# Softplus straight from PSUM and a stacked x projection, in the selective scan of a vision kernel

## The reference, cut to what matters

```
# xs: [B, 4, 256, L]; for each direction k
x_dbl  = x_proj_w[k] @ xs                    # 40 rows: 8 for the step, 16 B, 16 C
dt     = softplus(dt_proj_w[k] @ x_dbl[0:8] + dt_bias)      # the steps, 256 x L
B, C   = x_dbl[8:24], x_dbl[24:40]
h[t]   = exp(dt[t] * A) * h[t-1] + dt[t] * u[t] * B[t]      # 256 x 16 states
y[t]   = sum_n h[t, n] * C[t, n]  + D * u[t]
```

## Time and profile before

| | |
|---|---|
| time, median of 3 runs | 17439.1 us (17406.28 to 17441.4) |
| the profiled execution's own span | 17434.3 us |
| the scan's first and last Softplus table load | 5723.8 and 16927.9 us |
| ACT: Exp into a decay slot, mean of one | 772 ns |
| DVE: scan, mean of one | 1203 ns |

### The profile page before, as it was taken

The page is one execution under the profiler, slowest core; times in us unless marked ns, Lnnn a source line. Parts: engine busy times, 40 slices in busy tenths (PEclk is TensorE's granted clock), DMA queues, the critical chain, the costliest instruction groups (busy, mean ns, idle before and its releaser), DMA issues. The chain is left out here.

```text
span 17434.3 us, 303249 instructions
## 1 busy us (share of the span) xinstructions
PE 14999.7 (86%) x109786; PEld 10888.3 (62%) x109786; DVE 15172.8 (87%) x19332; ACT 14292.4 (82%) x28231; POOL 11441.1 (66%) x7881
## 2 busy tenths in 40 slices
PE   8999999997349788888888888888888888888888
PEld 5666666673113566666676676666666666666664
DVE  6777777347989899999999999999999999999995
ACT  5666666334545899999999999999999999999998
POOL 1111111000110799999999999999999999999998
PEclk9999999888679999999999999999999999999999
DMA  1000000112224333333333433333333333334336
GB/s 64 12 16 16 12 16 12 62 38 64 68 59 160 138 122 122 116 120 120 124 133 134 134 131 127 133 125 122 122 118 120 120 126 131 134 134 133 128 125 243
DMA packets 810527, 1801.57 MB, mean 103 GB/s; under 512 B 201328, under 2 KB 432208, under 8 KB 803280
## 3 DMA queue, kind: packets, MB, share of 16 engines
q1 hardware_dynamic: 809040, 1782.17, 30.4%
HBM read 1505.11 MB, written 276.82 MB: 102 GB/s over the span
## 5 line engine op out<-in xcount | busy, mean ns | idle before, releaser
L1832 DVE TENSOR_TENSOR_SCAN sc_h<-ps,sc_dBu 128x512 f32<-128x512 f32 x8192 | 9441.6, 1203 | 419.1 <-ACT ps L1699 396.4
L1803 POOL TENSOR_TENSOR sc_dBu<-sc_du,sc_Bb 128x2048 f32<-128x2048 f32 x2048 | 9310.9, 4546 | 9.0 <-DMA sc_Bb<-BD 7.6
L1699 ACT ACTIVATE ps<-sc_de,sc_A 128x512 f32<-128x512 f32 x8192 | 5920.5, 772 | 205.9 <-DVE sc_h L1832 195.6
L1666 PE MATMUL ps<-base,sc_h 128*128 128x128 f32 x32768 | 4637.4, 281 | 1493.9 <-DVE sc_h L1832 645.9
L1764 ACT ACTIVATE sc_hs<-ps,sc_CT 128x256 f32<-128x256 f32 x12288 | 5176.7, 553 | 154.9 <-PE ps L1666 115.3
L1666 PEld LDWEIGHTS ps<-base,sc_h 128*128 128x128 f32 x32768 | 3585.2, 142 | 2576.6 <-DVE sc_h L1832 2242.3
L1678 PE MATMUL ps<-base,sc_hs 128*128 128x128 f32 x32768 | 4344.7, 276 | 0.9 <-ACT sc_Yd L1771 0.4
L1678 PEld LDWEIGHTS ps<-base,sc_hs 128*128 128x128 f32 x32768 | 3704.4, 142 | 602.9 <-issue 496.2
L449 DVE CUSTOM_DVE_ANT_0 l_T<-ps,l_rel 128x512 f32<-128x512 f32 x2048 | 1329.0, 686 | 840.8 <-PE ps L357 840.8
L302 POOL TENSOR_SCALAR l_nm<-l_mx 128x1 f32<-128x1 f32 x1024 | 270.7, 279 | 2531.7 <-DVE l_mx L449 2531.7
L416 ACT ACTIVATE l_P<-l_T,l_nm 128x1024 f32<-128x1024 f32 x1024 | 1176.8, 1149 | 319.4 <-POOL l_nm L302 319.4
(11 more groups left out here) (252 smaller groups left out, 14651.6 us busy)
## 6 DMA issues: line engine op xcount, KB each, us to landing
sc_Bb<-BD SPq DMA_DIRECT2D x2048, 512.0 KB, 6.2
sc_u<-U SPq DMA_DIRECT2D x256, 512.0 KB, 4.6
Y<-sc_Yt SPq DMA_DIRECT2D x256, 512.0 KB, 3.3
U<-cv_u SPq DMA_DIRECT2D x32, 2048.0 KB, 13.1
sc_Yt<-Y SPq DMA_DIRECT2D x128, 512.0 KB, 8.6
gt_y<-Y SPq DMA_DIRECT2D x128, 512.0 KB, 8.6
l_raw<-in_x SPq DMA_DIRECT2D x72, 288.0 KB, 4.3
st_x<-in_x SPq DMA_DIRECT2D x8, 2048.0 KB, 15.6
```

What stands on the lines that cost most here:

```text
L1666: t = nc.tensor.transpose(hT[g][:, j, h * 128:(h + 1) * 128], h_[:, h, k * 128:(k + 1) * 128], d["ident"])
L1699: nc.scalar.activation(dA[q % 3], de[n % 2][:, h, s0 * SL:(s0 + 1) * SL], ACT.Exp, scale=par[pno(n) % 2][3][:, h, m:m + 1]).then_inc(ex_do ...
L1803: nc.gpsimd.tensor_tensor(dBu[x % 3], du[n % 2][:, :, s0 * SL:(s0 + 1) * SL].unsqueeze(1).broadcast_to([128, 2, 2, SL]), Bb[x % NBB].unsqu ...
L1832: nc.vector.tensor_tensor_scan(hr[P % 3][:, x % 2, h, ::step], dA[(2 * x + h) % 3][:, ::step], dBu[P % 3][:, x % 2, h, ::step], 0.0, ALU.m ...
```

## The change

- `x0` and `x1` become `xx` (unit 24). Both halves go into the one bank `xb`: half 0 in partitions 0 to 63, half 1 in partitions 64 to 127 (the weights are padded to 64 columns). One ACT copy of 128x512 takes both to `X`. `ct` then is 4 transposes of 128x128. The step weights `dtw` lie twice in SBUF, at partitions 0 and 64.
- The raw steps have no buffer any more: `tmp` and its four copies are gone. Softplus is four instructions of 512 columns, `p0` to `p3`, that read PSUM. `d0` and `d3` are still in `xb`; `d1` and `d2` are written into decay slots, which they take in turn with the exponentials (`ring_no`).
- All four matmuls now stand at the Softplus: `d0` in unit 12, `d1` behind the `fwd` of unit 13's list entry, `d2` and `d3` behind its `back`. On ACT `p0` to `p3` stand at the end of unit 12.

```diff
-    early = {22: "x0", 25: "x1", 28: "d0", 30: "d1"}
-    late = {1: "d2", 3: "d3", 7: "ct", 12: "sp"}
...
+        if s < NU and n + 2 < NC and m == 24:
+            order.append(("xx", n + 2))
+        if s < NU and n + 1 < NC and m == 7:
+            order.append(("ct", n + 1))
+        if s < NU and n + 1 < NC and m == 12:
+            order.append(("d0", n + 1))
+        if s < NU and n + 1 < NC and m == 13:
+            order.append(("d1", n + 1))
...
+        if s < NU and n + 1 < NC and m == 13:
+            order += [("d2", n + 1), ("d3", n + 1)]
...
+            if m == 12:
+                order += [(k, n + 1) for k in ("p0", "p1", "p2", "p3")]
...
                         for h in range(2):
-                            t = nc.tensor.matmul(xb[0:48, :], par[pno(x) % 2][0][:, h, :],
-                                                 ur[x % 3][:, h, q * SL:(q + 1) * SL], start=(h == 0), stop=(h == 1))
+                            for q in range(2):
+                                t = nc.tensor.matmul(xb[64 * q:64 * q + 64, :], par[pno(x) % 2][0][:, h, :],
+                                                     ur[x % 3][:, h, q * SL:(q + 1) * SL], start=(h == 0), stop=(h == 1))
...
+                        dt = slice(64 * q, 64 * q + 8)
+                        if kind in ("d0", "d3"):
+                            take(kind, x)
+                            dst, done = xb, xb_mm
+                        else:
+                            k = ring_no[x, int(kind[1])]
+                            if x:
+                                pe.wait_ge(sc_done, ring[k - 3] + 1)
+                            dst, done = dA[k % 3], rw_mm
+                        nc.tensor.matmul(dst, par[pno(x) % 2][1][dt, h * 128:(h + 1) * 128], X[dt, :],
+                                         start=True, stop=True).then_inc(done, 1)
...
-                        nc.scalar.copy(tmp[:, 0, q * SL:(q + 1) * SL], xb).then_inc(xb_act, 1)
...
-                        nc.vector.tensor_copy(tmp[:, 1, q * SL:(q + 1) * SL], xb).then_inc(xb_dve, 1)
...
+                        if i in (0, 3):
+                            act.wait_ge(xb_mm, xb_no["d%d" % i, x] + 1)
+                            raw = xb
+                        else:
+                            act.wait_ge(rw_mm, 2 * x + i)
+                            raw = dA[ring_no[x, i] % 3]
                         act.wait_ge(ex_done, 64 * (x - 1))
                         act.wait_ge(du_done, x - 1)
-                        for h in range(2):
-                            nc.scalar.activation(de[x % 2][:, h, :], tmp[:, h, :], ACT.Softplus,
-                                                 bias=par[pno(x) % 2][2][:, h, 16:17]).then_inc(sp_done, 1)
+                        nc.scalar.activation(de[x % 2][:, h, q * SL:(q + 1) * SL], raw, ACT.Softplus,
+                                             bias=par[pno(x) % 2][2][:, h, 16:17]).then_inc(sp_done, 1)
```

More of the change, by code:

```diff
@@ L1442, in scan_order @@
     for n in range(2):
[L1443 to L1447, removed]
+        order += [("fetch", n), ("xx", n), ("xx_", n), ("bst", n)]
         if n == 0:
-            order += [("e0", 0), ("du", 0)]
+            order += [(k, 0) for k in ("ct", "ct_", "d0", "d1", "d2", "d3", "p0", "p1", "p2", "p3", "e0", "du")]
     order += [("bb", P) for P in range(AHEAD)]
@@ L1495, in scan_order @@
         if s < NU and n + 2 < NC:
[L1496 to L1499, removed]
+            if m == 24:
+                order += [("xx_", n + 2), ("bst", n + 2)]
         if s < NU and n + 1 < NC:
-            if m in late:
-                order.append((late[m] + "_", n + 1))
+            if m == 7:
+                order.append(("ct_", n + 1))
+            if m == 12:
+                order += [(k, n + 1) for k in ("p0", "p1", "p2", "p3")]
             if m == 28:
@@ L1580, in _ @@
                             e.dma_start(xp.rearrange("p a b -> p (a b)"), I["xproj"][kk]).then_inc(par_ld[q % 2], 16)
-                            e.dma_start(dtw, I["dtw"][kk]).then_inc(par_ld[q % 2], 16)
+                            for i in range(2):
+                                e.dma_start(dtw[64 * i:64 * i + 8], I["dtw"][kk]).then_inc(par_ld[q % 2], 16)
                             e.dma_start(pc.rearrange("p a b -> p (a b)"), I["par"][kk]).then_inc(par_ld[q % 2], 16)
@@ L1640, in _ @@
                         h, q = divmod(int(kind[1]), 2)
[L1641 to L1644, removed]
+                        pe.wait_ge(xb_act, ended("xx", x))
+                        dt = slice(64 * q, 64 * q + 8)
+                        if kind in ("d0", "d3"):
+                            take(kind, x)
[7 more added lines that the diff above has]
+                                         start=True, stop=True).then_inc(done, 1)
                     elif kind in ("t0", "t1"):
@@ L1695, in exp @@
                     s0 = part(j)
-                    act.wait_ge(sp_done, 2 * n + 2)
+                    act.wait_ge(sp_done, 4 * n + 4)
                     act.wait_ge(a_ok, pno(n) + 1)
-                    act.wait_ge(sc_done, q - 2)
-                    nc.scalar.activation(dA[q % 3], de[n % 2][:, h, s0 * SL:(s0 + 1) * SL], ACT.Exp,
+                    k = ring_no[q]
+                    if k >= 3:
+                        old = ring[k - 3]
+                        if type(old) is int:
+                            act.wait_ge(sc_done, old + 1)
+                        else:
+                            act.wait_ge(sp_done, 4 * old[0] + old[1] + 1)
+                    nc.scalar.activation(dA[k % 3], de[n % 2][:, h, s0 * SL:(s0 + 1) * SL], ACT.Exp,
                                          scale=par[pno(n) % 2][3][:, h, m:m + 1]).then_inc(ex_done, 1)
```

79 lines of the change are left out of this document (38 added, 41 removed).

## The result

The changed kernel takes 17654.9 us (median of 4 runs, 17639.7 to 17675.0) against 17440.3 us (17406.3 to 17445.5) before: a ratio of 1.0129, 95% interval 1.0117 to 1.0140. It is 1.3% slower. The forecast was 17612 us, slower by 1.0%.

The account below looks back on a forecast made before the run. DVE was taken to bound the scan. Per chunk, -1.55 us of gain and +2.95 us of stall give +1.4 us, x 127 = +178 us; with some 5 us less in the first chunk, 17612 us (median), range 17440 to 17820.

Parts of the forecast that it names:

- DVE is the pacemaker; its waits decide: Scan: a chunk is DVE's own work plus 3.0 us of waiting for ACT; changes pay by cutting either.
- The stall at Softplus: End of unit 12: DVE's wait behind Softplus grows from 0.61 to 3.55 us, +2.95 us a chunk, mostly ACT waiting for PE.
- The pairs overlap: `d2` with `d3` take 1.13 us, the four x matmuls 1.9 us; rival without overlap: 17905 us, chance 0.08.
- The wait at unit 23: DVE's piece of unit 23: PE needs 5.55 us of 5.05 with `xx`, so DVE waits 0.5 us.
- Waits at units 26, 29 and 30 go: DVE's waits of 0.57 us at unit 26, 0.42 and 0.34 at units 29 and 30 disappear.
- What ACT can follow: Units 24 to 6: ACT limits the gain to 1.45 us in directions 0 and 1, 1.65 in 2 and 3; mean -1.55.
- the clock's rival: After the longer stall PE runs at 1.2 GHz in every chunk, 1 us a chunk more: 17740 us, chance 0.11.
- The pace: Scan: table loads, one Softplus a chunk, give 88.2 us a chunk.
- The total: Whole kernel: -1.55 + 2.95 = +1.4 us a chunk, +178 us over 127 chunks, 17612 us, +1.0%.

## Why the prediction was right, point by point

- **DVE is the pacemaker; its waits decide.** Right, with the limit shown by the kernel without DVE's copies: in directions 0 and 1 ACT sets the pace between units 24 and 6, and work taken from DVE alone comes back as a wait. The forecast's list of DVE's waits is not complete: there is one of 0.62 us at unit 14 in every chunk, before and after, and that of unit 26 is 0.80 us, not 0.57, in directions 0 and 1. The first changes nothing in the sum; the second made the forecast gain 0.1 us too small.
- **The stall at Softplus.** +2.95 us forecast, 3.75 - 0.61 = +3.14 measured. The places are those of the forecast: ACT waits for `d1` (1.31), then for the pair (1.39), where the forecast had near 1.2 each time. The missing 0.2 lies in PE's steps for the most part. Laid on the old times (the table loads are 10068.02 - 10020.74 = 47.28 us apart), `d1` begins at 22.87 where the forecast had 22.78, `p1` at 24.03 for 23.9, `p2` at 26.10 for 25.95, and DVE scans at 29.41 for 29.2. "Only some 0.2 are ACT's" was too little as well: the split costs 0.37 when ACT waits for nothing, as its own run shows. But in the changed kernel only `p2` and `p3` stand behind the last wait for PE, and they took 1.27 us where the forecast had 1.25, so the split is not the missing 0.2.
- **The pairs overlap.** Right at both places: 1.13 us for two raw steps, 1.98 when they share rows; 1.94 us for the four x matmuls.
- **The wait at unit 23.** +0.5 forecast, +0.90 measured, and moving `xx` took it away. The term was mis-sized: in the rows after, PE's steps are 1.16 for `fwd`, 1.87 for `xx`, 0.93, 0.86, and some 1.05 for the last `fwd`, 5.87 us, and DVE's four scans end 4.99 us after the first `fwd` began (10104.06 to 10109.05). I had 5.55 of 5.05. Most of the 0.3 is in the two `fwd`: 1.16 for my 0.96, and 1.05 for my 0.95. I had taken both from the time of unit 24, where PE ran behind other work; why they are longer here was not tried.
- **Waits at units 26, 29 and 30 go.** At 26 and 29 they went; 0.19 us stay at unit 30.
- **What ACT can follow.** The gain was forecast at 1.55 us. Measured is +2.0 for the whole and +3.14 for the stall, so a gain of 1.15 us, 0.4 short of the forecast. Against it stand the longer wait at unit 23 (0.4), a new one at unit 16, 0.24 us on average, which I had only under the clock's rival, and the 0.19 us at unit 30. For it stands that in directions 2 and 3 ACT kept up wholly, with no wait of DVE at units 5 and 6, where I had 0.4 us coming back (0.2 on the mean of the directions), and the 0.1 us of unit 26. In directions 0 and 1 0.76 us came back at unit 5, where I had 0.6. These terms add up to a shortfall of 0.6, not 0.4; the difference stays unexplained.
- **The clock.** A part of that rival came true: after the stall the transposes took 1.94 us at a granted clock of 0.50, the lower level, 1.2 GHz, in every chunk and not in 46 as before. A wait at unit 16 came with it, 0.45 us in 68 of the 127 chunks (before 0.18 us in 6). In the first 6 us in which DVE scans again, the mean granted clock was 0.63 in the chunks with this wait and 0.74 in those without; that the clock causes the wait is likely by this, not shown by a run. I had put 1 us a chunk on it, with 0.11; it measured 0.24.
- **The pace.** 88.2 us a chunk from the table loads was 0.3 too short: the first of them lies ahead of chunk 0, not in its unit 12. From the second on they give 88.5. Nothing hung on it.
- **The total.** +1.4 us a chunk forecast, +2.0 measured; the scan became 250 us longer, where the forecast had 178. That 17612 came so close to 17655 is in part luck: the stages ahead of the scan, which the change doesn't touch, were 33 us faster in the profiled run than in that of before. The mechanism, a stall at Softplus that outweighs what is saved, was right; the terms that were mis-sized are the gain (0.4) and the stall (0.2).

## What to carry to other kernels

A buffer between two engines is also what lets the first be late. Before taking it away, write down what stands ahead of the producing instruction in its own engine's order, and whether the consumer finds the value ready; here the same idea cost 1.3% where the values came late, and was part of a gain of 1.3% once only those that could be ready in time lost their buffer. Price the parts of such a gain one by one: in these kernels DVE's two copies alone were worth 47 us, and the stacked x projection in unit 22, which has nothing to do with the buffer, another 159. And when two engines are nearly level, find out per stretch which of the two is behind before choosing whose work to remove: the copies that were free to remove changed with the scan direction.

## What the runs showed of the hardware

Two matmuls of 8 rows and 512 columns ran wholly side by side from partitions 0 and 64 into different banks (1.13 us for both) and one after the other from the same partitions (1.98 us). Two matmuls of 64 columns with different moving data did so in the two halves of one bank (1.94 us for four). Putting this work on the path made the kernel depend on TensorE's clock: in 27 of 127 chunks of one kernel the granted clock stood at 1.2 GHz through a pair of raw steps (2.08 us instead of 1.13), and each of these chunks was 1.8 us longer. What makes it fall in these chunks and not in the others was not tried and stays open. Softplus over the same 2048 columns took 0.37 us longer in four instructions than in two, so each instruction has a fixed part of some (2.56 - 2.19) / 2 = 0.19 us, an estimate from these two rows. Changing ACT's function table took 1.28 us each time, with less than 0.02 us of idle time of ACT on either side of it.
